# A decoder layer on one core: four weight sums move to VectorE, one projection moves up in TensorE's order

## The chip, the cores and the metric

The kernel runs on one NeuronCore of a Trainium2 chip. The metric is the device time of one execution in microseconds. The engines are TensorE (PE), ScalarE (ACT), VectorE (DVE), GpSimd (POOL) and SyncE (SP), which issues every DMA of this kernel.

## What is computed

One decoder layer for 8 batches of 512 tokens and 256 channels:

```python
x = x + attn(layernorm(x))            # one head of 128; 512 keys
x = x + xattn(layernorm(x), ctx)      # relu(x W + b), relu(ctx W + b), masked softmax, times ctx
x = x + ffn(layernorm(x))             # 256 -> 1024 -> 256, quantised activations and weights

def weight_quant(w):                  # w_gate, w_up, w_down
    scale = 1.0 / clip(mean(abs(w)), 1e-5)
    return clip(round(w * scale), -1, 1) / scale
```

The change concerns `mean(abs(w))` of the three FFN weights, and the first three batches of `attn`.

## The kernel before

Each batch goes through three streams, in steps that have a letter and a batch number. `A` is self-attention: Q, K, V, VT (V transposed), S0 to S3 (scores of four groups of 128 queries), P0 to P3 (their exponentials transposed), H (P times V) and Y0, Y1 (H times the output weight, added to x). `E` projects the context: YP0 and YP1. `B` is cross-attention and `C` the FFN. `W` and `F` prepare weights: `F.sum0` to `F.sum5` sum |w| of the two halves of gate, up and down, `F.total` is the matmul with ones that adds them over the partitions (it needs all six), `F.sc` the small VectorE operations behind it, `F.round` and `F.sign` make the ternary weights on GpSimd and ScalarE.

The order of the work on every engine is written out by hand: `PE_ORDER`, `ACT_ORDER`, `DVE_ORDER`, `POOL_ORDER` and `SP_ORDER` are strings of steps, `run()` walks through them, and semaphores join the engines. An engine executes its list in order, so a step that waits holds up all that stands behind it in the list.

Exact products are made of two f32r halves. A step such as `A.Q/2` is six f32r matmuls on TensorE (L1070 to L1072); ScalarE then rounds the high half out of the PSUM bank (L835) and VectorE takes the low half (L1460); only then may the bank be filled again. Which bank an A or E step fills comes from `a_tables()`: a list of banks for the first steps, one for `A_NEXT` (the rest of the second batch), and then `a0` and `a1` in turn, while E steps from the third batch on use bank `e`:

```python
def a_step(step, n):
    dst = a_bank(step, n)
    if A_BEFORE[step, n]:
        a_read(*A_BEFORE[step, n])     # wait until the bank's last step has been read
```

Batch 0 differs: its x, context and W are used as they are loaded, without halves (`A.Q/0` is 4 matmuls in f32, `E.YP0/0` waits for the loads of W and of the context, L1158 on). Its key scale `r_bc` comes from a matmul `W.r` of a diagonal and ScalarE's copy (L848, `r0_set`), which the first score step and `A.V/0` on VectorE wait for. Every relu of YP (L888, L889) takes the bias, which comes with `W.o`, one load of 129.5 KB that also holds w_o and the head mask (`small_loaded`). VectorE's `W.wo0` (L1624) waits for the same load. For batch n > 0 `r_bc` goes by DRAM: SP stores a_rstd (`S.rw`) and loads it back to all partitions (`S.rb`).

The sum of one half of a weight is one ScalarE activation with an accumulator:

```python
def prep_sum(j):
    act.wait_ge(ffn_loaded[j // 2], 16)
    if j > 0:
        act.wait_ge(w_sums, j)
    act.activation(gateT..., ffn_raw[j // 2][:, ...], ACT.Abs,
                   accum_out=w_sum[:, j % 2, j // 2:j // 2 + 1]).then_inc(w_sums, 1)
```

Of the kernel before, what the change touches and what calls it, by code (L numbers as in the profile page):

```python
# [79 lines left out]
DVE_DN = [(n, t) for n in range(8) for t in range(4) if (n, t) not in POOL_DN]  # L80
SILU = [(6, j) for j in range(4, 8)] + [(7, j) for j in range(8)]
# [7 lines left out]
    A.P0/2 A.S2/2 B.P3/0 B.O2/0 A.P1/2 A.S3/2 B.O3/0 B.XT0/1 A.P2/2 A.P3/2 E.YP0/3 B.XT1/1 A.H/2 B.XP0/1 B.XP1/1
    E.YP1/3 A.Y0/2 A.Y1/2 C.g0/0 C.u0/0 A.Q/3 B.S0/1 B.S1/1 C.g1/0 C.u1/0 B.P0/1 B.S2/1 C.u2/0 C.g2/0 A.K/3  # L90
    A.V/3 B.P1/1 C.u3/0 C.g3/0 B.O0/1 B.S3/1 B.P2/1 C.g4/0 C.u4/0 E.YP0/4 C.g5/0 B.O1/1 C.u5/0 B.P3/1 B.O2/1
    A.VT/3 A.S0/3 B.O3/1 C.g6/0 C.u6/0 E.YP1/4 B.XT0/2 B.XT1/2 C.g7/0 C.DN0/0 C.u7/0 A.S1/3 A.P0/3 B.XP0/2
    B.XP1/2 A.S2/3 C.DN1/0 C.u0/1 C.g0/1 A.P1/3 A.S3/3 B.S0/2 B.S1/2 C.g1/1 C.u1/1 B.P0/2 B.S2/2 C.DN2/0 C.g2/1
    C.u2/1 C.DN3/0 B.P1/2 B.O0/2 A.P2/3 A.P3/3 C.g3/1 C.u3/1 B.S3/2 B.P2/2 C.g4/1 A.H/3 B.O1/2 B.P3/2 C.u4/1
    A.Y0/3 A.Y1/3 C.g5/1 C.u5/1 A.Q/4 A.K/4 C.u6/1 B.O2/2 B.O3/2 C.DN0/1 C.g6/1 B.XT0/3 B.XT1/3 A.V/4 E.YP0/5
    A.VT/4 A.S0/4 C.g7/1 C.u7/1 B.XP0/3 B.XP1/3 A.S1/4 A.P0/4 C.DN1/1 C.g0/2 A.S2/4 C.u0/2 C.DN2/1 A.P1/4 A.S3/4
    C.g1/2 C.u1/2 B.S0/3 B.S1/3 C.g2/2 C.u2/2 E.YP1/5 A.P2/4 A.P3/4 C.g3/2 C.u3/2 C.DN3/1 B.P0/3 B.S2/3 C.g4/2
    A.H/4 C.u4/2 B.P1/3 C.g5/2 B.O0/3 B.S3/3 A.Y0/4 A.Y1/4 B.P2/3 C.g6/2 C.u5/2 B.O1/3 B.P3/3 A.Q/5 A.K/5 C.u6/2
    B.O2/3 B.O3/3 A.V/5 B.XT0/4 B.XT1/4 C.g7/2 C.DN0/2 A.VT/5 A.S0/5 C.u7/2 B.XP0/4 C.DN1/2 A.S1/5 B.XP1/4
    A.P0/5 A.S2/5 C.u0/3 C.g0/3 C.DN2/2 C.u1/3 B.S0/4 C.g1/3 B.S1/4 A.P1/5 A.S3/5 B.P0/4 B.S2/4 C.g2/3 C.DN3/2  # L100
    C.u2/3 B.P1/4 B.O0/4 C.g3/3 B.S3/4 A.P2/5 A.P3/5 C.u3/3 B.P2/4 B.O1/4 C.u4/3 A.H/5 C.g4/3 E.YP0/6 A.Y0/5
    A.Y1/5 B.P3/4 C.u5/3 C.g5/3 B.O2/4 A.Q/6 A.K/6 B.O3/4 C.g6/3 C.u6/3 A.V/6 B.XT0/5 B.XT1/5 E.YP1/6 C.u7/3
    C.g7/3 A.VT/6 A.S0/6 B.XP0/5 C.u0/4 C.g0/4 B.XP1/5 C.DN0/3 C.g1/4 C.u1/4 C.DN1/3 A.S1/6 A.P0/6 B.S0/5 B.S1/5
    C.g2/4 A.S2/6 A.P1/6 B.P0/5 C.DN2/3 C.u2/4 A.S3/6 B.S2/5 C.u3/4 C.DN3/3 C.g3/4 B.P1/5 B.O0/5 A.P2/6 A.P3/6
    C.u4/4 C.g4/4 B.S3/5 B.P2/5 A.H/6 B.O1/5 C.g5/4 C.u5/4 A.Y0/6 A.Y1/6 B.P3/5 B.O2/5 C.g6/4 A.Q/7 A.K/7 C.u6/4
    B.O3/5 A.V/7 C.DN0/4 C.u7/4 A.VT/7 A.S0/7 B.XT0/6 B.XT1/6 E.YP0/7 C.g7/4 A.S1/7 A.P0/7 B.XP0/6 B.XP1/6
    A.S2/7 A.P1/7 C.g0/5 C.u0/5 C.DN1/4 A.S3/7 C.g1/5 B.S0/6 B.S1/6 A.P2/7 C.u1/5 A.P3/7 B.P0/6 B.S2/6 A.H/7
    C.g2/5 B.P1/6 B.O0/6 C.u2/5 A.Y0/7 A.Y1/7 C.u3/5 C.g3/5 B.S3/6 B.P2/6 E.YP1/7 C.g4/5 B.O1/6 C.u4/5 B.P3/6
# [7 lines left out]
    A.Q/0 W.qkv/0 W.hi/0 A.xT0/1 E.ctxT/1 A.xT1/1 W.r/0 E.YP0/0 A.VT/0 W.wo/0 F.sum0/0 A.exp0/0 A.exp1/0
    A.exp2/0 E.YP1/0 A.exp3/0 A.P0/0 A.Q/1 A.P2/0 A.K/1 F.sum1/0 F.sum2/0 E.YP0/1 A.xT0/2 A.xT1/2 F.sum3/0 A.H/0
    A.VT/1 F.sum4/0 F.sum5/0 A.exp0/1 E.YP1/1 A.P0/1 E.ctxT/2 A.exp1/1 A.exp2/1 A.exp3/1 A.P1/1 A.P2/1 A.P3/1
    B.mask/0 E.YP0/2 B.norm0/0 B.norm1/0 A.H/1 B.XT0/0 B.XT1/0 B.ctx/0 F.sign0/0 F.sign1/0 B.XP0/0 B.XP1/0
    E.YP1/2 A.Q/2 A.K/2 B.exp0/0 B.exp1/0 B.P0/0 E.ctxT/3 A.VT/2 B.P1/0 A.xT0/3 A.xT1/3 B.exp2/0 A.exp0/2 B.P2/0  # L120
    B.exp3/0 A.exp1/2 B.mask/1 A.P0/2 B.P3/0 B.norm0/1 B.norm1/1 A.P1/2 A.exp2/2 A.exp3/2 A.P2/2 A.P3/2
    C.norm0/0 B.XT0/1 B.XT1/1 F.sign2/0 F.sign3/0 E.YP0/3 F.sign4/0 A.H/2 F.sign5/0 B.XP0/1 B.XP1/1 C.t0/0
    C.u0/0 B.ctx/1 E.YP1/3 C.norm1/0 B.exp0/1 A.Q/3 C.t1/0 C.u1/0 B.P0/1 C.u2/0 C.t2/0 B.exp1/1 E.ctxT/4
    B.exp2/1 B.P1/1 B.norm0/2 A.K/3 C.t3/0 C.u3/0 A.xT0/4 B.P2/1 C.t4/0 B.exp3/1 B.mask/2 C.u4/0 C.hb0/0
    B.norm1/2 C.u5/0 B.P3/1 A.xT1/4 C.t5/0 E.YP0/4 C.norm0/1 A.VT/3 C.u6/0 C.t6/0 C.hb1/0 B.XT0/2 B.XT1/2
    A.exp0/3 C.t7/0 C.u7/0 A.P0/3 B.ctx/2 B.XP0/2 B.XP1/2 A.exp1/3 A.exp2/3 C.u0/1 C.t0/1 C.hb2/0 C.hb3/0
    B.exp0/2 C.t1/1 B.P0/2 C.u1/1 B.exp1/2 C.norm1/1 A.exp3/3 A.P1/3 B.exp2/2 B.P1/2 C.t2/1 C.u2/1 A.P2/3 A.P3/3
    C.t3/1 C.u3/1 E.ctxT/5 B.P2/2 C.t4/1 E.YP1/4 B.exp3/2 A.H/3 C.hb0/1 C.u4/1 C.u5/1 B.P3/2 C.norm0/2 A.Q/4
    A.K/4 C.t5/1 B.norm0/3 B.norm1/3 B.mask/3 B.XT0/3 B.XT1/3 C.t6/1 C.u6/1 C.hb1/1 C.hb2/1 A.VT/4 B.ctx/3
    C.t7/1 C.u7/1 A.exp0/4 B.XP0/3 B.XP1/3 A.P0/4 A.exp1/4 C.norm1/2 C.t0/2 C.u0/2 A.P1/4 E.YP0/5 C.t1/2 C.hb3/1  # L130
    C.u1/2 A.exp2/4 A.exp3/4 C.t2/2 C.u2/2 B.exp0/3 B.exp1/3 A.P2/4 A.P3/4 C.t3/2 C.u3/2 B.P0/3 C.t4/2 A.xT0/5
    A.xT1/5 A.H/4 C.u4/2 B.P1/3 C.t5/2 B.exp2/3 E.ctxT/6 C.hb0/2 B.P2/3 B.exp3/3 E.YP1/5 B.P3/3 C.u5/2 A.Q/5
    A.K/5 B.norm0/4 C.u6/2 B.mask/4 C.t6/2 B.norm1/4 C.hb1/2 B.XT0/4 B.XT1/4 C.norm0/3 C.t7/2 C.hb2/2 A.VT/5
    B.ctx/4 C.u7/2 A.exp0/5 B.XP0/4 B.XP1/4 A.P0/5 C.u0/3 C.t0/3 C.norm1/3 A.exp1/5 C.u1/3 C.hb3/2 B.exp0/4
    C.t1/3 A.xT0/6 A.xT1/6 B.P0/4 B.exp1/4 C.t2/3 A.P1/5 A.exp2/5 B.P1/4 A.exp3/5 B.exp2/4 C.t3/3 C.u2/3 A.P2/5
    A.P3/5 C.u3/3 B.P2/4 C.u4/3 B.exp3/4 A.H/5 B.mask/5 C.t4/3 C.norm0/4 C.hb0/3 C.hb1/3 C.t5/3 B.P3/4 E.YP0/6
    C.u5/3 A.Q/6 B.norm0/5 B.norm1/5 A.K/6 B.ctx/5 C.t6/3 C.u6/3 B.XT0/5 B.XT1/5 A.xT0/7 A.xT1/7 C.t7/3 A.VT/6
    C.u7/3 C.norm1/4 C.u0/4 C.t0/4 B.XP0/5 B.XP1/5 A.exp0/6 C.u1/4 C.t1/4 A.P0/6 C.hb2/3 C.hb3/3 A.exp1/6
    B.exp0/5 B.exp1/5 B.P0/5 C.t2/4 A.P1/6 C.u2/4 C.u3/4 A.exp2/6 A.exp3/6 C.t3/4 B.P1/5 A.P2/6 A.P3/6 B.exp2/5
    C.t4/4 C.hb0/4 C.u4/4 E.YP1/6 B.P2/5 A.H/6 E.ctxT/7 C.t5/4 B.exp3/5 B.P3/5 C.u5/4 B.mask/6 C.t6/4 A.Q/7  # L140
# [1583 lines left out]
```

## Time and profile before

| | |
|---|---|
| time, median of 3 runs | 372.63 us (371.84 to 372.91) |
| the profiled execution: its time, its span | 372.06 us, 370.1 us |
| busy: PE, ACT, DVE, POOL | 98%, 86%, 85%, 79% of the span |
| TensorE clock granted | full (1.0) |
| DMA | 36.92 MB, mean 100 GB/s |
| chain that ended last | PE 76%, POOL 6%, ACT 5%, DMA 4%, DVE 3% |

The span runs from the first to the last instruction of the profiled execution; the time of that execution is 1.96 us longer. Timeline rows give the start and the duration of an instruction (or of some merged ones, x their number) and in brackets how long the engine sat idle before it and what released it. Busy time of a pipelined matmul includes overlap with the next one: successive 128x512 f32r matmuls start 0.23 us apart though each is shown as 0.39 us long.

### The profile page before, as it was taken

The page shows a single profiled execution, that of the slowest core. Times are in us where ns is not written, and L with a number is a line of the kernel's source. Part 1 is how long each engine was busy: PE and PEld are TensorE (multiplying, and loading weights), DVE is VectorE, ACT ScalarE, POOL GpSimd, SP SyncE. Part 2 cuts the span into 40 slices and gives each one's busy share as a digit, 9 for nine tenths or more (in the row PEclk, how much of TensorE's full clock was granted, in tenths as well). Part 3 has the DMA queues.
Part 4 walks back from the last instruction along what each step waited for, and adds up shares of the span by engine and source line. Part 5 has one row for each costly group of instructions (what it writes and reads, how often), then busy time and mean ns, then how long its engine had stood idle before and what let it go on. Part 6 is the DMA issues. An engine that isn't in the chain of part 4 may idle for free.

```text
span 370.1 us, 7362 instructions
## 1 busy us (share of the span) xinstructions
PE 361.5 (98%) x2116; PEld 280.2 (76%) x2116; DVE 313.8 (85%) x918; ACT 318.6 (86%) x590; POOL 294.0 (79%) x421
## 2 busy tenths in 40 slices
...
DMA packets 47735, 36.92 MB, mean 100 GB/s; under 512 B 39248, under 2 KB 40912, under 8 KB 47312
## 3 DMA queue, kind: packets, MB, share of 16 engines
...
q14 instruction: 22, 0.18, 0.2%
...
## 4 chain that ended last, share of the span: by engine, by line
PE 76%; POOL 6%; ACT 5%; DMA 4%; DVE 3%; issue 3%; SPq 1%; POOLq 0%; ACTq 0%; DVEq 0%
PE b_bank L1070 8%; PE b_bank L1071 8%; PE b_bank L1072 8%; PE a_bank L1070 6%; PE a_bank L1072 6%; PE a_bank L1071 6%; PE g_bank L1284 5%; PE d_bank L1304 5%; PE u_bank L1284 5%; PE b_bank L1212 3%; DMA x_all<-in_x 2%; PE a_bank L1132 2%; PE b_bank L1183 2%; POOL c_work L703 1%; POOL xp_lo L656 1%
## 5 line engine op out<-in xcount | busy, mean ns | idle before, releaser
L703 POOL TENSOR_TENSOR c_work<-c_work 128x512 f32<-128x512 f32 x48 | 61.8, 1297 | 3.4 <-DVE c_work L1540 2.4
L960 ACT ACTIVATE c_work<-g_bank,c_tanh_scale 128x512 f32<-128x512 f32 x52 | 35.9, 690 | 5.8 <-PE g_bank L1284 3.3
L1070 PE MATMUL b_bank<-ctx_hi,b_pT_hi 128*128 128x256 f32 x128 | 39.2, 307 | 0.0
L1540 DVE SCALAR_TENSOR_TENSOR c_work<-c_work,g_bank 128x512 f32<-128x512 f32 x50 | 33.9, 678 | 6.1 <-ACT c_work L960 5.7
L1071 PE MATMUL b_bank<-ctx_lo,b_pT_hi 128*128 128x256 f32 x128 | 36.1, 282 | 0.0
L1072 PE MATMUL b_bank<-ctx_hi,b_pT_lo 128*128 128x256 f32 x128 | 36.0, 282 | 0.0
L963 ACT ACTIVATE c_work<-u_bank 128x512 f32<-128x512 f32 x48 | 28.9, 601 | 8.2 <-PE u_bank L1284 8.2
L1284 PE MATMUL g_bank<-gateT,xqT 128*128 128x512 bf16 x112 | 33.6, 382 | 0.9 <-ACT xqT L935 0.5
L750 POOL TENSOR_SCALAR c_work<-c_work,h_q 128x1024 f32<-128x1024 f32 x28 | 31.7, 1132 | 3.2 <-DVE h_q L1574 3.2
L1284 PE MATMUL u_bank<-upT,xqT 128*128 128x512 bf16 x112 | 33.5, 381 | 0.6 <-DVE c_work L1535 0.6
L1567 DVE TENSOR_REDUCE h_max<-c_work 128x1 f32<-128x1024 f32 x26 | 31.4, 1206 | 1.1 <-POOL c_work L703 1.1
L1304 PE MATMUL d_bank<-downT,c_half 128*128 128x256 bf16 x240 | 31.2, 273 | 0.2 <-DMA c_half<-c_half 0.2
L1304 PEld LDWEIGHTS d_bank<-downT,c_half 128*128 128x128 bf16 x240 | 22.7, 98 | 8.5 <-issue 2.7
L651 POOL TENSOR_TENSOR yp_lo<-e_relu,yp_hi 128x512 fp32r<-128x512 f32 x16 | 20.7, 1295 | 10.2 <-ACT yp_hi L889 10.2
L970 ACT ACTIVATE c_half<-c_work 128x1024 bf16<-128x1024 f32 x26 | 27.3, 1056 | 0.5 <-POOL c_work L750 0.5
L1070 PE MATMUL b_bank<-yp_hi,xp_hi 128*128 128x512 f32 x64 | 27.4, 429 | 0.1
L1070 PEld LDWEIGHTS b_bank<-ctx_hi,b_pT_hi 128*128 128x128 f32 x128 | 24.3, 190 | 1.8 <-issue 0.2
L643 POOL TENSOR_TENSOR a_xT_lo<-a_xT_raw,a_xT_hi 128x512 fp32r<-128x512 f32 x14 | 18.4, 1316 | 8.6 <-ACT a_xT_hi L844 8.6
L1072 PE MATMUL b_bank<-yp_hi,xp_lo 128*128 128x512 f32 x64 | 25.2, 394 | 0.0
L898 ACT ACTIVATE b_p<-b_p,b_nmax 128x512 f32<-128x512 f32 x32 | 23.1, 723 | 2.5 <-DVE b_nmax L1516 2.4
L1071 PE MATMUL b_bank<-yp_lo,xp_hi 128*128 128x512 f32 x64 | 25.1, 391 | 0.0
L1516 DVE CUSTOM_DVE_ANT_0 b_p<-b_bank,mask_add 128x512 f32<-128x512 f32 x32 | 21.8, 683 | 3.7 <-PE b_bank L1072 3.6
...
## 6 DMA issues: line engine op xcount, KB each, us to landing
ctx_raw<-in_ctx SPq DMA_DIRECT2D x8, 512.0 KB, 4.5
a_xT_raw<-in_x_t SPq DMA_DIRECT2D x7, 512.0 KB, 4.4
ctxT_raw<-in_ctx_t SPq DMA_DIRECT2D x7, 512.0 KB, 5.4
x_all<-in_x SPq DMA_DIRECT2D x7, 512.0 KB, 3.8
out<-x_all SPq DMA_DIRECT2D x7, 512.0 KB, 2.9
...
c_work<-in_w_gate SPq DMA_DIRECT2D x1, 1024.0 KB, 10.9
c_work<-in_w_up SPq DMA_DIRECT2D x1, 1024.0 KB, 12.6
```

The costliest lines, as they stand in the source:

```text
L703: pool.tensor_tensor(h[:, t % 2, half * HALF:(half + 1) * HALF], th[:, j % 2, :], up[:, j % 2, :], ALU.mult).then_inc(hs, 1)
L750: pool.tensor_scalar(h_tile(t, n), h_tile(t, n), h_q[:, t:t + 1], ROUND if n < LAST else ROUND_F16, ALU.mult, ALU.add).then_inc(h_rounds, 1)
L960: act.activation(gate_tile(j, n), gu_bank("g", j, n), ACT.Silu if (n, j) in SILU else ACT.Tanh, scale=c_tanh_scale[:, j // 2:j // 2 + 1]). ...
L963: act.activation(up[:, j % 2, :], gu_bank("u", j, n), ACT.Copy).then_inc(ups, 1)
L970: act.activation(h_q8[:, t % 2, :], h_tile(t, n), ACT.Copy, bias=-ROUND).then_inc(hqs, 1)
L1070: pe.matmul(dst, l_hi, r_hi, start=first, stop=False)
L1071: pe.matmul(dst, l_hi, r_lo, start=False, stop=False)
L1072: return pe.matmul(dst, l_lo, r_hi, start=False, stop=last)
L1284: mm = pe.matmul(dst, xqT[:, t * DC + c, :], w[:, c, cols], start=c == 0, stop=c == DC - 1)
L1304: mm = pe.matmul(dn_bank(t, n)[:, 0:D], h_T[:, t % 2, f, :], downT[:, f, :], start=f == 0, stop=f == FC - 1)
L1540: dve.scalar_tensor_tensor(gate_tile(j, n), gate_tile(j, n), 1.0, gu_bank("g", j, n), ALU.add, ALU.mult).then_inc(gates, 1)
L1567: dve.tensor_reduce(h_max[:, one], h_tile(t, n), AX.X, ALU.max, apply_absolute_value=True).then_inc(h_maxes, 1)
```

## The change

Four of the six sums (up and down) become VectorE reductions with their own semaphore; `F.total` waits for both. `A.Q/2` enters `A_NEXT` between `P1/1` and `P2/1` and fills bank `e`, and with it the turn of `a0` and `a1` is shifted by one for all later A steps. The five order strings are written anew over roughly the first third of the work; from there to the end they are as before.

```diff
-A_NEXT = "S3/1 P1/1 P2/1 P3/1 H/1 Y0/1 Y1/1"
+A_NEXT = "S3/1 P1/1 Q/2 P2/1 P3/1 H/1 Y0/1 Y1/1"
-SECOND_BANKS = ["u", "d", "a0", "a1", "g", "u", "d"]
+SECOND_BANKS = ["u", "d", "e", "a0", "a1", "g", "u", "d"]
     later = [f"{step}/{n}" for n in range(2, 8) for step in A_STEPS.split()]
+    later = [entry for entry in later if entry not in A_NEXT.split()]
+DVE_SUMS = [2, 3, 4, 5]
+ACT_SUMS = [m for m in range(6) if m not in DVE_SUMS]
...
             def prep_sum(j):
                 act.wait_ge(ffn_loaded[j // 2], 16)
-                if j > 0:
-                    act.wait_ge(w_sums, j)
+                if ACT_SUMS.index(j) > 0:
+                    act.wait_ge(w_sums, ACT_SUMS.index(j))
...
                 elif name == "total":
-                    pe.wait_ge(w_sums, 6)
+                    pe.wait_ge(w_sums, len(ACT_SUMS))
+                    pe.wait_ge(dve_w_sums, len(DVE_SUMS))
...
+            def prep_sum(j):
+                dve.wait_ge(ffn_loaded[j // 2], 16)
+                dve.tensor_reduce(w_sum[:, j % 2, j // 2:j // 2 + 1], ffn_raw[j // 2][:, (j % 2) * F:(j % 2 + 1) * F], AX.X, ALU.add,
+                                  apply_absolute_value=True).then_inc(dve_w_sums, 1)
```

In step names: on ScalarE `A.exp1/1` now follows `A.exp0/1` directly (two sums, `E.YP1/1`, `A.P0/1` and `E.ctxT/2` stood before it), `B.mask/0` and `B.ctx/0` come ahead of `A.exp0/1`, and the first `E.YP0/0` stands before `A.exp0/0`. On GpSimd the a_rstd steps of batch 1 come ahead of `E.ctxT/1`. On SP `S.ctx/0`, `S.ctxT/2` and `S.xT/2` stand between `S.rw/1` and `S.rb/1`.

The start of SyncE's list, the loads in the order in which they are issued (`wo_and_small` is the load with the bias, `b_xn` here holds the transposed context of batch 0, `a_xT_raw`, `ctxT_raw` and the second `x_all` belong to batch 1). Before:

```order
L580 DMA x_all<-in_x 128x512 x2
L591 DMA wo_and_small<-in_w_o_b_mask 128x259
L587 DMA xqT<-in_W 128x512
L585 DMA b_xn<-in_ctx_t 128x1024
L524 DMA a_xT_raw<-in_x_t 128x1024
L543 DMA ctxT_raw<-in_ctx_t 128x1024
L550 DMA mask_u8<-in_mask 128x512
L512 DMA x_all<-in_x 128x1024
L594 DMA c_work<-in_w_gate 128x2048
L594 DMA c_work<-in_w_up 128x2048
```

Now:

```order
L582 DMA x_all<-in_x 128x512
L552 DMA mask_u8<-in_mask 128x512
L582 DMA x_all<-in_x 128x512
L589 DMA xqT<-in_W 128x512
L526 DMA a_xT_raw<-in_x_t 128x1024
L514 DMA x_all<-in_x 128x1024
L545 DMA ctxT_raw<-in_ctx_t 128x1024
L587 DMA b_xn<-in_ctx_t 128x1024
L596 DMA c_work<-in_w_gate 128x2048
L593 DMA wo_and_small<-in_w_o_b_mask 128x259
L596 DMA c_work<-in_w_up 128x2048
```

The mask went between the halves of batch 0's x, batch 1's x went up by two large loads, the context of batch 0 went down by two, and the bias load went behind gate.

VectorE around `A.V/0` (`vT<-g_bank`) and the first scores (the ISA rows), with `W.wo0` (`hm_f`). Before:

```order
L1631 TENSOR_TENSOR wt_lo<-xqT,wt_hi 128x512
L1624 CAST hm_f<-wo_and_small 128x1
L1355 BN_STATS a_bn<-x_all 128x6 x4
L1491 TENSOR_TENSOR vT<-g_bank,r_bc 128x512
L1362 BN_AGGR a_mv<-a_bn 128x2 x2
L1479 ISA a_p,a_max<-e_bank,r_bc,a_rstd 128x512
L1479 ISA a_max 128x1
L1479 ISA a_p,a_max<-b0_bank,r_bc,a_rstd 128x512
```

Now:

```order
L1358 BN_STATS a_bn<-x_all 128x6 x4
L1365 BN_AGGR a_mv<-a_bn 128x2 x4
L1482 ISA a_p,a_max<-e_bank,r_bc,a_rstd 128x512
L1482 ISA a_max 128x1
L1494 TENSOR_TENSOR vT<-g_bank,r_bc 128x512
L1639 TENSOR_TENSOR wt_lo<-xqT,wt_hi 128x512
L1632 CAST hm_f<-wo_and_small 128x1
L1482 ISA a_p,a_max<-b0_bank,r_bc,a_rstd 128x512
```

The first score of batch 0 stands ahead of `A.V/0`, and `hm_f`, which needs the bias load, between the first and the second score. The sums of `up` follow after the fourth score, those of `down` after `A.P3/0`.

TensorE around `A.P1/1`, the first transpose row in each. Before:

```order
L1132 MATMUL d_bank<-ident,a_p 128x128 x4
L1327 MATMUL b1_bank<-w_sum,ones 128x3 x2
L1132 MATMUL a0_bank<-ident,a_p 128x128 x4
L1132 MATMUL a1_bank<-ident,a_p 128x128 x4
L1070 MATMUL e_bank<-ctxT_hi,wt_hi 128x512
L1071 MATMUL e_bank<-ctxT_lo,wt_hi 128x512
```

Now:

```order
L1134 MATMUL d_bank<-ident,a_p 128x128 x4
L1072 MATMUL e_bank<-a_xT_hi,wqkv_hi 128x512
L1073 MATMUL e_bank<-a_xT_lo,wqkv_hi 128x512
L1074 MATMUL e_bank<-a_xT_hi,wqkv_lo 128x512
L1072 MATMUL e_bank<-a_xT_hi,wqkv_hi 128x512
L1073 MATMUL e_bank<-a_xT_lo,wqkv_hi 128x512
L1074 MATMUL e_bank<-a_xT_hi,wqkv_lo 128x512
L1134 MATMUL a0_bank<-ident,a_p 128x128 x4
L1330 MATMUL b1_bank<-w_sum,ones 128x3 x2
L1134 MATMUL a1_bank<-ident,a_p 128x128 x4
L1072 MATMUL e_bank<-ctxT_hi,wt_hi 128x512
```

The six matmuls of `A.Q/2` stand behind `A.P1/1`, and `E.YP0/2` (the last row) fills the same bank `e` behind them.

## Rows read from the trace of the kernel before

**Rows 1.** The page: span, and busy time of each engine
```profile
span 370.1 us, 7362 instructions
PE 361.5 (98%) x2116; PEld 280.2 (76%) x2116; DVE 313.8 (85%) x918; ACT 318.6 (86%) x590; POOL 294.0 (79%) x421
```

**Rows 2.** TensorE's timeline: start, duration, operation, idle before and releaser
```profile
17.37 0.66 PE L1116 MATMUL u_bank<-ident,vT 128*128 128x128 f32 x4 [1.01 <-DVE vT L1491]
...
21.30 0.60 PE L1132 MATMUL e_bank<-ident,a_p 128*128 128x128 f32 x4
...
39.74 0.63 PE L1132 MATMUL d_bank<-ident,a_p 128*128 128x128 f32 x4 [1.05 <-ACT a_p L867]
...
41.53 0.48 PE L1070 MATMUL e_bank<-ctxT_hi,wt_hi 128*128 128x512 f32 x1
...
42.55 0.40 PE L1071 MATMUL e_bank<-ctxT_lo,wt_hi 128*128 128x512 f32 x1
42.78 0.39 PE L1072 MATMUL e_bank<-ctxT_hi,wt_lo 128*128 128x512 f32 x1
43.55 0.47 PE L1070 MATMUL g_bank<-a_pT_hi,b_pT_hi 128*128 128x512 f32 x1 [0.38 <-DVE a_pT_lo L1464]
...
137.17 0.60 PE L1284 MATMUL g_bank<-gateT,xqT 128*128 128x512 bf16 x2 [0.21 <-DMA xqT<-xq]
```

**Rows 3.** ScalarE's timeline
```profile
13.01 1.06 ACT L919 ACTIVATE ctxT_hi<-ctxT_raw 128x1024 fp32r<-128x1024 f32 x1 [0.59 <-DMA ctxT_raw<-in_ctx_t]
...
14.49 0.58 ACT L848 ACTIVATE r_bc<-b_bank 128x512 f32<-128x512 f32 x1
...
18.96 1.04 ACT L859 ACTIVATE gateT<-c_work 128x1024 f32<-128x1024 f32 x1
...
20.00 0.71 ACT L867 ACTIVATE a_p<-a_p,a_nmax 128x512 f32<-128x512 f32 x1
...
35.52 0.71 ACT L867 ACTIVATE a_p<-a_p,a_nmax 128x512 f32<-128x512 f32 x1
...
38.79 0.72 ACT L867 ACTIVATE a_p<-a_p,a_nmax 128x512 f32<-128x512 f32 x1
```

**Rows 4.** VectorE's timeline
```profile
16.64 0.67 DVE L1491 TENSOR_TENSOR vT<-g_bank,r_bc 128x512 f32<-128x512 f32 x1
...
24.09 0.18 DVE L1656 RECIPROCAL a_inv<-a_sum 128x4 f32<-128x4 f32 x1 [2.99 <-ACT a_p L867]
...
32.88 0.69 DVE L1468 TENSOR_TENSOR hT_lo<-d_bank,hT_hi 128x512 fp32r<-128x512 f32 x1 [4.57 <-ACT hT_hi L838]
...
42.13 1.28 DVE L1464 TENSOR_TENSOR a_pT_lo<-a_bank,a_pT_hi 128x512 fp32r<-128x512 f32 x2
...
55.32 0.69 DVE L1460 SCALAR_TENSOR_TENSOR q_lo<-a_bank,q_hi 128x512 fp32r<-128x512 f32 x1 [1.37 <-ACT q_hi L835]
```

**Rows 5.** SyncE's timeline: when loads were issued
```profile
5.70 0.44 SPq L550 DMA_DIRECT2D mask_u<-in_mask  x1
6.19 0.65 SPq L512 DMA_DIRECT2D x_all<-in_x  x1
6.88 0.71 SPq L594 DMA_DIRECT2D c_work<-in_w_gate  x1
7.63 0.44 SPq L594 DMA_DIRECT2D c_work<-in_w_up  x1
```

**Rows 6.** DMA issues of 0 to 30 us: KB each, median us to landing
```profile
c_work<-in_w_gate SPq DMA_DIRECT2D x1, 1024.0 KB, 10.9
c_work<-in_w_up SPq DMA_DIRECT2D x1, 1024.0 KB, 12.6
...
x_all<-in_x SPq DMA_DIRECT2D x1, 512.0 KB, 9.1
...
mask_u<-in_mask SPq DMA_DIRECT2D x1, 64.0 KB, 7.9
```

**Rows 7.** The page's groups: busy, mean ns, idle before
```profile
L1567 DVE TENSOR_REDUCE h_max<-c_work 128x1 f32<-128x1024 f32 x26 | 31.4, 1206 | 1.1 <-POOL c_work L703 1.1
```

More of the change, by code:

```diff
@@ L89 @@
[L89 to L108, printed above, removed]
```

232 lines of the change are left out of this document (126 added, 106 removed).

## The prediction

> **What bounds the kernel now.** I read the page first. TensorE is busy 361.5 of 370.1 us, and no other engine passes 86% [rows 1]. A busy share alone doesn't prove a bound, so the second view is TensorE's timeline, row by row. Inside a step the f32r matmuls start 0.23 us apart (42.55, 42.78) though each is drawn 0.39 us long [rows 2]: the drawn length includes 0.16 us of overlap, and the next matmul is always there to start. The third view is the list of TensorE's waits. Between 16 us and 137 us it has three entries: 1.01 us before 17.37 (the transpose of V of batch 0, released by VectorE), 1.05 us before 39.74 (`A.P1/1`, released by ScalarE's exponential) and 0.38 us before 43.55 (`A.H/1`, released by VectorE); the next is 0.21 us at 137.17 [rows 2]. The chain of waits agrees: 76% of it is TensorE.
>
> So the change, which takes no work from TensorE, can win only what TensorE waits, or lose by new waits. The ceiling: 1.01 + 1.05 + 0.38 = 2.44 us, and at each wait the 0.16 us of overlap is lost too, 0.48 us: **2.9 us**. All of it lies ahead of 44 us.
>
> The Trainium skill, Perfetto Trace Analysis, Identifying the Most-Contended Engine, says that matmul busy time is a bad measure of TensorE's headroom and that the busy share of weight loads should be used instead; by it there would be room here. The weight loads are at 76% [rows 1]. I hold with the spacing of the starts; what the other reading would give is a rival below.
>
> **Part 1: the loads and the start of batch 0.** The first wait of TensorE is for `A.V/0` on VectorE, which ran at 16.64 for 0.67 us [rows 4], behind the statistics of batch 1's x. That x landed at 6.19 + 9.1 = 15.3 us [rows 5, 6], though the scale `r_bc` that V needs was ready at 14.49 + 0.58 = 15.07 [rows 3]. Now batch 1's x is issued two large loads earlier. Loads land nearly in the order of issue: gate at 6.88 + 10.9 = 17.8, up at 7.63 + 12.6 = 20.2, so 1024 KB take 2.4 us and 512 KB 1.2 us [rows 5, 6]; x should land near 12 and its statistics be done by 14. Then `r_bc` decides. Ahead of its copy ScalarE has the same kinds of work as before (the transposed context of batch 1, which waited for its load until 13.01, and one 128x512 copy), so 15.07 stands if that load does. VectorE then takes the first score (0.68, about the 0.67 of V's row) and V, both at 0.6 to 0.7 us: done at about 16.4 instead of 17.3, a gain of 0.9 us.
>
> Against it stands the mask, now ahead of all large loads. It landed at 5.70 + 7.9 = 13.6, which is 0.6 us behind the context load of 13.01, and the x behind it needed 1.7 us more instead of 1.2 [rows 3, 5, 6]. So mask and x can bring 0 to 1.0 us of delay to whatever stands behind them, the context of batch 1 among them. I take 0.3: **gain 0.6 us**, bounds -0.1 and 0.9.
>
> The bias load moves behind gate. The bytes up to its end are those up to gate's end before, so it should land at about 17.8 to 18.0. ScalarE's two relus of `E.YP0/0` (two 128x512 passes, 1.2 us together) then end at 19.2 and the first exponential starts there, against 20.00 before, when `F.sum0` (18.96 to 20.00, 1.04 us) stood in that place [rows 3]. TensorE's `A.P0/0` stood at 21.30 [rows 2], would now stand at 20.7 and needs the exponential, done at 19.9: 0.8 us of cover. VectorE's `hm_f` waits for the same load, and the second score, at about 18.0 in both orders, behind it.
>
> **Part 2: the sums.** A reduction of 128x1024 on VectorE costs 1.21 us [rows 7], four cost 4.8 us; ScalarE gives up four of 1.04 us [rows 3]. The sums of up stand where VectorE was idle 2.99 us before 24.09, those of down where it was idle 4.57 us before 32.88 [rows 4]. The first pair can start when up has landed (20.2) and the fourth score is done (about 20.5) and pushes the copy of `A.P1/0` to some 23.4 to 24.1, where it was; the second ends near 29.5. TensorE needs nothing of VectorE in between but `A.V/1`, for the transpose behind `A.H/0`, at about 31. Cost: **0**. If that cover is gone (V/1 also waits for the reload of `r_bc`, which now has three loads of 512 KB ahead of it, 3.6 us behind the weights' end at about 22.6, so some 26.3 and the broadcast itself), each us beyond 30.3 costs one. On ScalarE 4.2 us go, but it is not the bound: **0** by itself.
>
> **Part 3: batch 1 and the moved Q.** `A.exp1/1` came at 38.79, 3.27 us behind `A.exp0/1` at 35.52 [rows 3], because four steps stood between. Now it follows at once, so the 1.05 us wait of `A.P1/1` goes. What is late next is VectorE. From 32.88 (`hT_lo`) to 42.13 + 1.28 = 43.41 (the low halves of P2 and P3) it works almost without a pause, 10.5 us, and all of it hangs on `A.H/0` [rows 4]. Its list keeps all this work and gets the low half of Q/2, 0.69 us in its row [rows 4], 0.6 between starts. With the gain g of part 1 it ends at 44.0 - g; the half of Q/2, which stands ahead of those of P2 and P3 (1.2 us), at 42.8 - g. On TensorE Q/2 takes 6 x 0.23 = 1.4 us. It fills the time of the old wait, but `E.YP0/2` fills the same bank `e` behind it and has to wait for VectorE: from 42.8 - g to 44.2 - g. Then `A.H/1` starts; P3's half is there. Before, H/1 started at 43.55 and Q/2 was still to come. Gain: 43.55 + 1.4 - (44.2 - g) = **0.75 + g**. So of the 1.4 us that the moved Q could hide about half is given back as a new wait of 0.5 to 1.2 us on bank `e`. Q/2's place behind `A.Y1/1` is taken by V/2, which needs nothing new.
>
> **Part 4: the rest to the end.** The reordered stretch reaches to about 115 us, and behind it the lists are as before. TensorE had no wait from 44 to 137 us, and the steps that feed it have 1.4 us less to come in. ScalarE is better placed there (sums gone; context, mask and sign steps earlier), VectorE as before. I count 0, with bounds of -0.5 and +0.3 (the waits at 137 and in the tail).
>
> **Sum:** 0.75 + 0.6 = 1.35 us. The profiled execution took 372.06 us (span 370.1 and 1.96 around it) and would take 370.7. The median of the runs is 0.57 us above the profiled one, so the forecast for the median is 372.63 - 1.35 = **371.3 us**, with a range of its own from 370.6 (g at its upper bound, tail +0.3) to 372.0 (g near 0).
>
> **Rivals.**
> 1. *Both waits vanish and none comes.* For it: ScalarE's exponentials are much earlier. Against it: VectorE's 10.5 us run. It gives the ceiling, 372.63 - 2.9 = 369.7 us. Chance 0.15.
> 2. *The waits only move.* The mask costs the whole 1.0 us (g = -0.1), and the new waits on P2/1, P3/1 and bank `e` take most of the rest. 372.63 - 0.4 = 372.2 us. For it: the mask's row. Chance 0.17.
> 3. *TensorE was not the bound, ScalarE was.* Then the four sums come off the time: 4 x 1.04 = 4.2, giving 368.4 us. Against it: TensorE's starts are 0.23 us apart without a gap. This is what the page cited above would suggest. Chance 0.03.
> 4. *Slower: the bias load comes late.* It stands behind the 1024 KB of gate in a full queue. If it lands at t, the exponential is done at t + 1.9 and `A.P0/0` starts then, so g = 21.3 - (t + 1.9) = 19.4 - t as soon as t passes 18.8, and the gain is 20.15 - t. It decides from t = 20.15, which is up's landing; landing with down (about 22.6) it costs 2.45 us: 375.1 us. For it: `hm_f` and the relus both block lists. Against it: other loads landed in order. Chance 0.10.
>
> **How the numbers follow.** The forecast has 0.55. A measurement of this kernel can tell about 0.3%, 1.1 us, from no change, so faster means below 371.5. The forecast's own range lies on that side for 0.6 of its weight: 0.33, and rivals 1 and 3 add 0.18: faster 0.51. Slower by over 0.3% (above 373.7) is rival 4 past t = 21.3, and some room for a wait that I don't see: 0.09. The same: 0.40. The range runs from 369.7 (rival 1) to 373.0, which takes in rival 2 and the mild end of rival 4; about 0.15 is left out.
>
> **What would show it.** In the changed profile: TensorE's transposes of V/0 start 0.5 to 1.0 us earlier with a wait that is short or gone; `A.P0/0` near 20.7; the wait for ScalarE's exponential before `A.P1/1` is gone; a new wait of 0.5 to 1.2 us before `E.YP0/2`, released by VectorE's low half of Q; `A.H/1` near 43.6 with Q/2 done; four reductions of 1.2 us on VectorE without anyone waiting; landing of the bias by 18.8. Wrong would be: a wait of VectorE or ScalarE for the bias beyond that, a wait of TensorE on `A.V/1`'s transpose (the reload), or new waits of TensorE between 50 and 130 us.

## The result and the profile after

The changed kernel takes **373.69 us** (median of 20 runs, 372.05 to 374.75), the kernel before 372.13 us beside it (20 runs, 371.09 to 375.31). The ratio is 1.0033, with a 95% interval from 1.0017 to 1.005: slower by 1.2 us, by the medians by 1.56 us, where I had forecast a gain of 1.35 us. The profiled execution has a span of 371.7 us against 370.1.

The page of the changed kernel, the lines that answer to [rows 1]:

```profile
span 371.7 us, 7326 instructions
PE 360.4 (97%) x2088; PEld 280.6 (75%) x2116; DVE 319.1 (86%) x922; ACT 314.5 (85%) x582; POOL 294.0 (79%) x421
```

TensorE's timeline of the changed kernel (it answers to [rows 2]; L1082 is `A.V/0`, L1324 `W.r`, the first L1134 row `A.P0/0`, the second `A.P1/1`, L1072 into bank `e` `E.YP0/2`, L1072 into `g` `A.H/1`):

```profile
11.72 1.98 PE L1082 MATMUL g_bank<-c_xn,b_p 128*128 128x512 f32 x4 [1.73 <-DVE b_p L1622]
15.26 1.13 PE L1324 MATMUL b_bank<-vT,ones 128*128 128x512 f32 x2 [1.56 <-DVE vT L1370]
...
23.53 0.60 PE L1134 MATMUL e_bank<-ident,a_p 128*128 128x128 f32 x4
...
40.78 0.60 PE L1134 MATMUL d_bank<-ident,a_p 128*128 128x128 f32 x4
...
44.79 0.49 PE L1072 MATMUL e_bank<-ctxT_hi,wt_hi 128*128 128x512 f32 x1 [0.42 <-DVE q_lo L1463]
...
46.29 0.39 PE L1072 MATMUL g_bank<-a_pT_hi,b_pT_hi 128*128 128x512 f32 x1
```

The second half of this is what was forecast: the wait before `A.P1/1` is gone, a short one on bank `e` has come. The first half is not. `A.V/0` and `W.r`, which no term of my sum touches, are late. The same two steps before:

```profile
9.33 1.98 PE L1080 MATMUL g_bank<-c_xn,b_p 128*128 128x512 f32 x4
11.80 1.13 PE L1322 MATMUL b_bank<-vT,ones 128*128 128x512 f32 x2 [0.48 <-DVE vT L1367]
```

So `A.V/0` starts 2.39 us late and `W.r` 3.46 us. VectorE's timeline of the changed kernel says why in its first row: the statistics of the second half of batch 0's x wait 2.18 us for its load. The centring of V's weights (`b_p`, L1622) stands behind them in VectorE's list, and `A.V/0` waits for that. (Before this wait the matmuls of Q and K start 0.49 us late, at 6.39 instead of 5.90. That is scatter: of two kernels below that differ in nothing up to there, one starts them at 5.63 and one at 6.64.)

```profile
10.26 0.75 DVE L1358 BATCH_NORM_STATS2 a_bn<-x_all 128x6 f32<-128x256 f32 x2 [2.18 <-DMA x_all<-in_x]
10.93 0.37 DVE L1365 BATCH_NORM_AGGREGATE a_mv<-a_bn 128x2 f32<-128x6 f32 x4
11.21 0.46 DVE L1622 SCALAR_TENSOR_TENSOR b_p<-u_bank,b_p 128x128 f32<-128x128 f32 x2
...
13.45 1.75 DVE L1370 TENSOR_TENSOR vT<-ident,a_rstd 128x512 f32<-128x512 f32 x1
```

The last row is a second surprise: the spread of the scales, which feeds `W.r`, takes 1.75 us. Before, it took 0.69, and all four statistics were one row at 7.22:

```profile
7.22 1.41 DVE L1355 BATCH_NORM_STATS2 a_bn<-x_all 128x6 f32<-128x256 f32 x4 [1.08 <-DMA x_all<-in_x]
...
11.06 0.69 DVE L1367 TENSOR_TENSOR vT<-ident,a_rstd 128x512 f32<-128x512 f32 x1
```

SyncE's timeline of the changed kernel: the mask is issued at 2.58, and the issue at 4.47 takes 2.19 us, its neighbours 0.43.

```profile
2.58 0.43 SPq L552 DMA_DIRECT2D mask_u<-in_mask  x1
3.05 0.43 SPq L582 DMA_DIRECT2D x_all<-in_x  x1
...
4.47 2.19 SPq L514 DMA_DIRECT2D x_all<-in_x  x1
```

Its stretches of 1 us (busy time of PE, PEld, DVE, ACT, POOL with instructions, granted clock, DMA share, GB/s): three slices at 216, 172 and 286 GB/s.

```profile
5.00:6.00 1.00, 1.00 (x7) 1.00 (x6) 0.57 (x3) 0.00 (x0) 0.00 (x0) 1.00 0.69 216
6.00:7.00 1.00, 1.00 (x6) 0.76 (x6) 0.40 (x2) 0.00 (x0) 0.00 (x0) 1.00 0.65 172
7.00:8.00 1.00, 1.00 (x3) 0.40 (x3) 0.68 (x2) 0.00 (x0) 0.00 (x0) 1.00 0.83 286
```

The kernel before has 358, 235 and 331 GB/s there.

From this came **theory M**: the mask's load, 512 bytes that go to all 128 partitions, holds up what is behind it by some 2 us. **Theory P**: the long spread comes from GpSimd, which takes the low halves of xT/1 (batch 1's transposed x) meanwhile. The rival to both: the sums, the moved Q or VectorE's long run cost the time, and the late start is only a shift.

### The profile page after: what moved, and what is told of

It reads as the page before. It is cut to its first block, busy times and chain, and to the rows that moved or that the text cites. A ratio compares the mean times of both kernels' runs of the same rounds, so it can differ in the third digit from the quotient of the medians.

```text
span 371.7 us, 7326 instructions
## 1 busy us (share of the span) xinstructions
PE 360.4 (97%) x2088; PEld 280.6 (75%) x2116; DVE 319.1 (86%) x922; ACT 314.5 (85%) x582; POOL 294.0 (79%) x421
## 4 chain that ended last, share of the span: by engine, by line
PE 81%; POOL 4%; ACT 4%; DMA 4%; DVE 3%; issue 3%; SPq 1%; ACTq 0%; POOLq 0%; DVEq 0%
PE b_bank L1072 9%; PE b_bank L1074 9%; PE b_bank L1073 9%; PE a_bank L1074 6%; PE a_bank L1072 6%; PE a_bank L1073 6%; PE g_bank L1286 5%; PE u_bank L1286 5%; PE d_bank L1306 5%; PE b_bank L1214 3%; PE a_bank L1134 2%; DMA x_all<-in_x 2%; PE b_bank L1185 2%; PE e_bank L1072 2%; PE e_bank L1073 2%
## 5 line engine op out<-in xcount | busy, mean ns | idle before, releaser
L1072 PE MATMUL b_bank<-ctx_hi,b_pT_hi 128*128 128x256 f32 x128 | 39.3, 307 | 0.0
L1286 PE MATMUL u_bank<-upT,xqT 128*128 128x512 bf16 x103 | 31.6, 381 | 1.1 <-DVE c_work L1538 0.6
L1286 PE MATMUL g_bank<-gateT,xqT 128*128 128x512 bf16 x93 | 29.4, 381 | 2.1 <-ACT xqT L937 0.5
L1072 PE MATMUL b_bank<-yp_hi,xp_hi 128*128 128x512 f32 x64 | 28.0, 437 | 0.1
L1072 PEld LDWEIGHTS b_bank<-ctx_hi,b_pT_hi 128*128 128x128 f32 x128 | 24.3, 190 | 2.3 <-issue 0.6
L1073 PEld LDWEIGHTS b_bank<-ctx_lo,b_pT_hi 128*128 128x128 f32 x128 | 24.4, 190 | 0.5
L869 ACT ACTIVATE a_p<-a_p,a_nmax 128x512 f32<-128x512 f32 x32 | 23.1, 728 | 1.5 <-DVE a_nmax L1487 1.4
```

Of the source, the lines that this page charges most:

```text
L1072: pe.matmul(dst, l_hi, r_hi, start=first, stop=False)
L1073: pe.matmul(dst, l_hi, r_lo, start=False, stop=False)
L1286: mm = pe.matmul(dst, xqT[:, t * DC + c, :], w[:, c, cols], start=c == 0, stop=c == DC - 1)
```

## The experiments

Each kernel ran 12 times (the one called "the same row" 6 times) and was timed against the kernel before on its own chip; ratios are those. The medians of the kernel before were 371.95 us beside mask late, mask alone, no overlap and bias in the slot; 371.83 beside distinct rows, Q back, sums back and both repairs; 372.11 beside the same row, the mask on ScalarE's queue, sums alone and Q's low half first. The profile is of one execution, and its time can lie 1.3 us off the median; where it does, the text says so.

### Undoing one part at the start

**Mask late.** The changed kernel with

```diff
-    W.x0/0 S.mask/0 W.x1/0 W.W/0 S.xT/1 S.x/1 S.ctxT/1 W.c/0 F.gate/0
+    W.x0/0 W.x1/0 W.W/0 S.xT/1 S.x/1 S.ctxT/1 W.c/0 S.mask/0 F.gate/0
```

> The changed kernel with only the mask's load moved: from between the two halves of x0 to behind the bias c, ahead of gate. Theory M (the mask's load, which writes one 512-byte row to each of 128 partitions, holds up whatever stands behind it by some 2 us, and with x0's second half the centring of V, the transposes of A.V/0, the scale row W.r and A.P0/0): x0's second half lands by 8.3 us instead of 10.26, A.V/0 starts on TensorE by 9.6 instead of 11.7, W.r near 12.5 instead of 15.3, A.P0/0 near 21 instead of 23.5, and the time falls by 2.2 to 2.9 us below the changed kernel, to 370.8 to 371.5, below the kernel before. Rival (the sums, the moved Q or VectorE's long run are the cost and the start is only shifted): within 0.5 us of the changed kernel, 373.2 to 373.9.

Measured: 370.92 us, ratio 0.9967 (0.9948 to 0.9986). TensorE's timeline:

```profile
9.88 1.88 PE L1082 MATMUL g_bank<-c_xn,b_p 128*128 128x512 f32 x4
...
21.41 0.63 PE L1134 MATMUL e_bank<-ident,a_p 128*128 128x128 f32 x4
```

`A.V/0` starts 1.84 us earlier than in the changed kernel, without a wait, and `A.P0/0` 2.12 us. Both are 0.3 to 0.4 us behind what I expected; the spread still takes 1.75 us. Moving one load of 64 KB gives back 2.5 us by the ratios, and what is left of the change beats the kernel before. The rival that the start is only a shift falls.

**The mask alone**, in the kernel before:

```diff
-    W.x0/0 W.x1/0 W.o/0 W.W/0 W.c/0 S.xT/1 S.ctxT/1 S.mask/0 S.x/1
+    W.x0/0 S.mask/0 W.x1/0 W.o/0 W.W/0 W.c/0 S.xT/1 S.ctxT/1 S.x/1
```

> The kernel before with one edit: the mask's load moved ahead of x0's second half, as in the changed kernel. Theory M: x0's second half lands near 10.2 us instead of 7.7, the first transposes of V start near 11.7 instead of 9.3, and the time rises by 2.0 to 2.8 us, to 374.2 to 375.0. Rival (the mask's place costs only in company with the rest of the new load order): within 0.5 us of the kernel before, 371.7 to 372.6.

Measured: 372.31 us, ratio 1.0002 (0.9981 to 1.0023). That is the rival's range, and theory M's 2.0 to 2.8 us are not there. The start is late all the same. TensorE's timeline (of the slowest of the 12 executions, 373.57 us):

```profile
11.21 1.98 PE L1080 MATMUL g_bank<-c_xn,b_p 128*128 128x512 f32 x4 [1.14 <-DVE b_p L1614]
13.68 1.12 PE L1322 MATMUL b_bank<-vT,ones 128*128 128x512 f32 x2 [0.49 <-DVE vT L1367]
...
18.07 0.60 PE L1116 MATMUL u_bank<-ident,vT 128*128 128x128 f32 x4
```

`A.V/0` and `W.r` are 1.88 us late, but the wait of 1.01 us before the transpose of V [rows 2] is gone: batch 1's x lands late there anyway, and the late start runs into that slack. `A.P0/0` stands at 21.95, 0.65 us behind. So the mask holds up the loads in both kernels, and what that costs depends on the rest of the order of loads, as the rival said. The change brought batch 1's x earlier and put the mask in front with the same edit, so it had no such slack left to cover the mask.

**No overlap.** The changed kernel with a wait ahead of GpSimd's first low half of xT/1:

```diff
                 pool.wait_ge(xT_his, DC * (n - 1) + c + 1)
+                if n == 1 and c == 0:
+                    pool.wait_ge(r0_spread, 1)
```

> The changed kernel with one wait added: GpSimd's low halves of xT/1 (128x512 each, 1.6 us) start only when VectorE has spread the scales (the operation at 13.45 us that took 1.75 us where it took 0.69 before). Theory P (the two engines' overlap made it long): it takes 0.7 us, W.r starts near 14.2 instead of 15.26, the time falls by about 1.0 us against the changed kernel, to 372.7. Rival (it is long for a reason of its own, or something behind it takes the gain): it still takes over 1.5 us and the time stays within 0.3 us of the changed kernel. The halves of xT/1 end later by about 1 us, at 17.5, ahead of their first user on TensorE by more than that, so no loss is expected from them.

Measured: 371.78 us, ratio 0.9985 (0.9964 to 1.0005), 1.8 us below the changed kernel by the ratios, where I expected 1.0. In the profiled executions the spans are 1.4 us apart (370.3 and 371.7) and `A.P0/0` is 1.32 us earlier, 0.25 of which is the load, 10.01 instead of 10.26. VectorE's and GpSimd's timelines:

```profile
13.20 0.68 DVE L1372 TENSOR_TENSOR vT<-ident,a_rstd 128x512 f32<-128x512 f32 x1
```
```profile
14.03 2.51 POOL L647 TENSOR_TENSOR a_xT_lo<-a_xT_raw,a_xT_hi 128x512 fp32r<-128x512 f32 x2 [1.43 <-DVE vT L1372]
```

In the changed kernel GpSimd's pair had begun 0.31 us ahead of the spread, and both were slow together, 3.20 instead of 2.51 and 1.75 instead of 0.68:

```profile
13.14 3.20 POOL L645 TENSOR_TENSOR a_xT_lo<-a_xT_raw,a_xT_hi 128x512 fp32r<-128x512 f32 x2 [0.29 <-ACT a_xT_hi L846]
```

### What about the mask holds the queue

**Bias in the slot.** Mask late, and the bias load (129.5 KB, 128 rows too) in the mask's place:

```diff
-    W.x0/0 S.mask/0 W.x1/0 W.W/0 S.xT/1 S.x/1 S.ctxT/1 W.c/0 F.gate/0 W.o/0 F.up/0
+    W.x0/0 W.o/0 W.x1/0 W.W/0 S.xT/1 S.x/1 S.ctxT/1 W.c/0 S.mask/0 F.gate/0 F.up/0
```

> As the kernel with the mask late (mask behind c), but the bias load of W.o, whose rows are longer, stands in the slot between x0's halves that the mask had. If the count and the small size of the mask's descriptors are what holds the queue: x0's second half lands by 8.5 us and the time is within 0.3 us of the mask-late kernel. If any load in that slot costs as much: x0's second half lands beyond 9.3 us and the time is within 0.6 us of the changed kernel.

Measured: 371.04 us, ratio 0.9967 (0.9946 to 0.9988); x0's second half is used at 8.28, as expected. Neither the slot nor the bytes are the cost.

**Distinct rows.** Mask late plus one more load in the slot, into a tile that nothing reads:

```diff
+                elif name == "d":
+                    sp.dma_start(spare[:, :], w_gate[:, 0, 0:P]).then_inc(spare_loaded, 16)
```

> The mask-late kernel (370.92 us) with one load added in the slot between x0's halves: 64 KB in 128 rows of 512 bytes, as the mask's, but read from 128 different places of w_gate; it writes a tile that nothing reads. If what holds the queue is that the mask's 128 rows are all read from the same 512 bytes: x0's second half lands by 8.4 us and the time is 370.7 to 371.4. If rows of 512 bytes in themselves do: it lands beyond 9.3 us and the time is 372.4 to 373.9.

Measured: 371.02 us, ratio 0.9976 (0.9958 to 0.9995). The statistics start at 6.68 and run through without a wait for the second half. By the ratios this is 0.3 us above mask late, less than the intervals can tell: 128 rows of 512 bytes have no price here that shows.

**The same row.** The same kernel, except for the source:

```diff
-                    sp.dma_start(spare[:, :], w_gate[:, 0, 0:P])...
+                    sp.dma_start(spare[:, :], w_gate[0, 0, 0:P].partition_broadcast(P))...
```

> The mask-late kernel (370.92 us) with a 64 KB load in the slot between x0's halves, as in the distinct-rows kernel (371.02 us), except that all 128 rows are read from the same 512 bytes of w_gate. Theory S (128 reads of one place of the memory hold the queue): x0's second half lands at 9.3 us or later, A.V/0 starts beyond 11 us, and the time is 372.3 to 373.9. Rival (something of the mask itself, its type or its tensor): x0's second half by 8.4 us, 370.7 to 371.4.

Measured: 374.22 us, ratio 1.006 (1.0039 to 1.0081), by the medians 3.2 us above the distinct rows. VectorE's timeline has the wait again:

```profile
9.62 0.75 DVE L1362 BATCH_NORM_STATS2 a_bn<-x_all 128x6 f32<-128x256 f32 x2 [1.85 <-DMA x_all<-in_x]
```

The DMA issues of 0 to 30 us, KB and us to landing, of the distinct rows and then of the same row:

```profile
spare<-in_w_gate SPq DMA_DIRECT2D x1, 64.0 KB, 4.3
```
```profile
spare<-in_w_gate SPq DMA_DIRECT2D x1, 64.0 KB, 6.4
```

The two kernels differ in nothing but whether 128 reads of 512 bytes go to 128 places or to one. That decides: 2.1 us later to land, and 3.2 us in time. It is not a matter of more pieces, both profiles count 3025 packets from 0 to 30 us; where in the memory or the DMA engines the repeated reads are held is not shown. The Trainium skill, DMA: Bandwidth & Descriptors, Rules for kernel authors, advises to join many small transfers into a large one, since under 64 KB one pays mostly overhead. That goes by size, and the two loads have the same size, 64 KB: it can't tell 4.3 us from 6.4, so it is not what made the mask dear.

**The mask on ScalarE's queue**, issued at that engine's start:

```diff
+            act.dma_start(mask_u8[:, 0, :], mask[0, :].partition_broadcast(P)).then_inc(mask_loaded, 16)
```

> The changed kernel with the mask's load issued from ScalarE's queue at its start instead of SP's. If the mask blocks only what stands behind it in the same queue: x0's second half lands by 8.3 us and the time is 370.6 to 371.5, as with the mask late. If it takes the memory or the DMA engines for as long as it runs: some load of the start is late by 1 us or more again, A.V/0 starts beyond 10.8 us, and the time is over 372.

Measured: 373.51 us, ratio 1.0034 (1.0016 to 1.0053). x0 is in time for everything, but now the first load of all is late; TensorE's timeline (of the fastest of the 12 executions, 372.16 us, so it can't account for the whole of the median):

```profile
5.98 1.19 PE L1320 MATMUL b_bank<-b_p,ones 128*128 128x128 f32 x4 [2.08 <-DMA b_p<-in_w_qkv]
```

`w_qkv` lands at 0.72 + 5.1 = 5.8 us instead of 3.7, and the two loads of `c_xn` behind it take 5.4 us instead of 3.9. So the load doesn't only block what stands behind it in its own queue: loads that move at the same time on SyncE's queue are late by 1.5 to 2.1 us.

### The other two parts

**Q back.** The bias-slot kernel with `A.Q/2` at its old place and `A_NEXT` and `SECOND_BANKS` as before:

```diff
-    A.P1/1 A.Q/2 A.P2/1 F.total/0 ... A.Y1/1 A.K/2
+    A.P1/1 A.P2/1 F.total/0 ... A.Y1/1 A.Q/2 A.K/2
```

> The bias-slot kernel (371.04 us) with Q/2 back at its old place behind Y1/1, in its old bank. Theory Q (the prediction's part 3: the moved Q fills TensorE's time between A.P1/1 and A.H/1, in which VectorE's low halves are late): a wait of 0.5 to 1.4 us comes back on TensorE ahead of A.P2/1, A.P3/1 or A.H/1, and the time rises by 0.4 to 1.2 us, to 371.4 to 372.2. Rival (the exponential's new place alone made the gain, the moved Q only shifts work): within 0.3 us of 371.04.

Measured: 373.32 us, ratio 1.0028 (1.001 to 1.0047), 2.3 us above the bias-slot kernel by the ratios. TensorE has its wait again, now one step on, before `A.P2/1`:

```profile
39.85 0.63 PE L1132 MATMUL a_bank<-ident,a_p 128*128 128x128 f32 x4 [1.52 <-ACT a_p L867]
```

From `A.P1/1` (1.07 us earlier than in the bias-slot kernel, 37.74 against 38.81) to `A.H/1` with Q/2 counted in (42.82 + 1.4 = 44.2 against 44.31) this costs 1.0 us. Up to there the earlier start pays for it. Another 1.1 us are lost behind, a little in a wait of 0.20 us at 55.54, so that the spans are 1.0 us apart (370.8 against 369.8). The medians are 2.3 us apart, about twice the most I expected, and I have no row for all of it.

The start of this profiled execution shows theory P without an edit of GpSimd's work. VectorE's spread came first, by 0.12 us:

```profile
10.62 0.68 DVE L1368 TENSOR_TENSOR vT<-ident,a_rstd 128x512 f32<-128x512 f32 x1
```
```profile
10.74 2.94 POOL L643 TENSOR_TENSOR a_xT_lo<-a_xT_raw,a_xT_hi 128x512 fp32r<-128x512 f32 x2 [0.72 <-ACT a_xT_hi L844]
```

Now VectorE is at its 0.68 and GpSimd pays, 2.94 us instead of 2.51. The Trainium skill, SBUF — State Buffer, Who interferes with whom, has this as a rule: a VectorE instruction with two inputs in SBUF contends with a GpSimd instruction that reads SBUF, the port pair that they share is an exclusive lock, and the order of issue decides who is blocked. The traces agree: in the changed kernel VectorE's excess, 1.07 us, is about what GpSimd's running instruction had left (half of the undisturbed 2.51 is 1.26 us, 0.31 were gone, which leaves 0.95), and GpSimd's excess, 0.69 us, is the length of VectorE's instruction.

**Sums back.** The bias-slot kernel with all six sums on ScalarE, at their old places:

```diff
-DVE_SUMS = [2, 3, 4, 5]
+DVE_SUMS = []
-    F.sum1/0 E.YP0/1 A.xT0/2 A.xT1/2 B.mask/0 A.H/0 A.VT/1 B.ctx/0 A.exp0/1
+    F.sum1/0 F.sum2/0 E.YP0/1 A.xT0/2 A.xT1/2 F.sum3/0 B.mask/0 A.H/0 A.VT/1 F.sum4/0 F.sum5/0 B.ctx/0 A.exp0/1
```

> The bias-slot kernel (371.04 us) with all six sums of |w| on ScalarE again, the four at the places they had in the kernel before. Theory (part 2 of the prediction: the sums cost nothing on either engine by themselves): within 0.3 us of 371.04. Rival A (the four sums on ScalarE, 4.2 us, push its exponentials of batch 1 behind TensorE's need): a wait of TensorE on ScalarE of 0.5 us or more between 24 and 41 us and a time over 371.5. Rival B (the sums on VectorE cost time in the changed kernel): below 370.6.

Measured: 373.15 us, ratio 1.0031 (1.001 to 1.0051), 2.4 us above the bias-slot kernel by the ratios: rival A. TensorE's timeline has three stalls, two of them for ScalarE's exponential:

```profile
34.30 0.35 PE L1070 MATMUL u_bank<-wo_hi,hT_hi 128*128 128x256 f32 x1 [0.74 <-issue]
...
38.03 0.63 PE L1132 MATMUL a_bank<-ident,a_p 128*128 128x128 f32 x4 [0.70 <-ACT a_p L867]
...
42.50 0.63 PE L1132 MATMUL a_bank<-ident,a_p 128*128 128x128 f32 x4 [0.60 <-ACT a_p L867]
```

**Sums alone.** The kernel before with the four sums on VectorE and nothing else moved:

```diff
-    A.N3/0 A.inv/0 A.P1/0 A.Q/1 A.K/1 A.P3/0 A.V/1
+    A.N3/0 F.sum2/0 F.sum3/0 A.inv/0 A.P1/0 A.Q/1 A.K/1 A.P3/0 F.sum4/0 F.sum5/0 A.V/1
```

> The kernel before with one part of the change: four of the sums on VectorE, at the places where it was idle, nothing else moved. Theory A (from the run with the sums back: ScalarE's sums are what made its exponential of batch 1 late): TensorE's wait of 1.05 us before A.P1/1 goes or halves, and the time falls by 0.3 to 1.2 us, to 370.6 to 371.5. Rival (part 2 of the prediction: the sums are worth nothing by themselves, the order of the exponentials is): the wait stays at about 1 us and the time within 0.3 us of the kernel before.

Measured: 372.82 us, ratio 1.002 (0.9997 to 1.0044). No gain: by the ratio 0.7 us above the kernel before, outside the rival's 0.3, but the interval reaches down to no change. The rival's mechanism holds, TensorE's wait has not moved:

```profile
40.41 0.63 PE L1131 MATMUL d_bank<-ident,a_p 128*128 128x128 f32 x4 [1.04 <-ACT a_p L866]
```

Together: moving the sums is worth nothing where `A.exp1/1` stands behind three other steps (the prediction miscounted them as four), and 2.4 us where it follows at once and the mask and context steps are ahead of it. The move of the sums and the new order of ScalarE are one measure; neither is priced alone.

### Towards a better version

**Both repairs**: bias in the slot, mask late, and the no-overlap wait.

> The bias-slot kernel (mask behind c, bias load in its old slot, 371.04 us) with the wait of the no-overlap kernel added: GpSimd's low halves of xT/1 start when VectorE has spread the scales. Theory P (the overlap with GpSimd costs the chain 1.07 us): the spread takes 0.7 us instead of 1.75, W.r starts near 12.2 instead of 13.28, A.P0/0 near 20.5 instead of 21.55, the time is 0.8 to 1.1 us lower, 369.9 to 370.2. Rival (something else, as the context of batch 1 on ScalarE, holds the scale row's copy then): A.P0/0 gains less than 0.4 us and the time stays above 370.6.

Measured: **370.38 us**, ratio 0.9952 (0.9929 to 0.9974), the lowest of all, below the kernel before by 1.8 us by the ratio and by 1.45 by the medians. Against bias in the slot it is 0.6 us by the ratios, less than the 0.8 to 1.1 expected, and the two intervals overlap, so the second repair shows in the times only on top of the changed kernel. In the profile it shows here too: the spread takes 0.68 us and `A.P0/0` stands at 20.20 instead of 21.55:

```profile
12.04 1.02 PE L1326 MATMUL b_bank<-vT,ones 128*128 128x512 f32 x2
...
20.20 0.60 PE L1136 MATMUL e_bank<-ident,a_p 128*128 128x128 f32 x4
```

The first matmuls of Q and K, in bias in the slot and then in both repairs, which have the same work up to there, show how much a single start can scatter:

```profile
5.63 3.76 PE L1082 MATMUL a_bank<-c_xn,b_p 128*128 128x512 f32 x8
```
```profile
6.64 3.84 PE L1084 MATMUL a_bank<-c_xn,b_p 128*128 128x512 f32 x8
```

**Q's low half first**, in that kernel:

```diff
-    A.P1/1 B.ag1/0 A.Q/2 A.P2/1
+    A.Q/2 A.P1/1 B.ag1/0 A.P2/1
```

> The kernel with the bias slot and without the overlap (370.38 us, the best so far) with VectorE's low half of Q/2 moved ahead of those of P1/1. TensorE's wait of 0.42 us on bank e before E.YP0/2 should shrink or go; at most 0.42 + 0.16 = 0.6 us lower, 369.8 to 370.2, if nothing takes its place. Rival: the low half of Q/2 now waits for TensorE's Q/2 and holds P1/1's, P2/1's and P3/1's behind it, A.H/1 waits instead, and the time stays at 370.2 to 370.8.

Measured: 370.87 us, ratio 0.9973 (0.9957 to 0.9989), no gain. The wait grew from 0.42 to 1.01 us, and VectorE now idles 0.76 us for ScalarE's high half of Q:

```profile
41.37 0.50 PE L1073 MATMUL e_bank<-ctxT_hi,wt_hi 128*128 128x512 f32 x1 [1.01 <-DVE a_pT_lo L1468]
```

It is released by the low half of P1/1, not of Q: the kernel has TensorE wait for a count of low halves, Q/2's place in TensorE's order, so the place in VectorE's list doesn't bring the release forward. The edit didn't test what I meant it to.

## Why the prediction was wrong

**What bounds the kernel: right.** TensorE does. ScalarE gave up 4.1 us and the time rose, so rival 3 is out.

**Part 1: this step failed.** "So mask and x can bring 0 to 1.0 us of delay to whatever stands behind them, the context of batch 1 among them", of which I took 0.3. The delay is 2.39 us, read at `A.V/0`; moving the mask away took 1.84 of it, and the other 0.55 is of the size of the scatter of the first matmuls. I bounded it by the landings of the mask where it stood before, which say how long it took, not what it held up; around 13.6 us the kernel before loses no throughput (419 GB/s from 13 to 14 us). And I took the context of batch 1 as what stands behind it, though the rows of the order show the second half of x0 directly there. ScalarE's copy `r_bc` was done at 17.03 (16.43 + 0.60), not at 15.1 to 15.4 [rows 3]. The path that I did watch was late by far more than 0.3 us too. ScalarE's timeline:

```profile
14.66 1.06 ACT L921 ACTIVATE ctxT_hi<-ctxT_raw 128x1024 fp32r<-128x1024 f32 x1 [0.60 <-DMA ctxT_raw<-in_ctx_t]
...
16.43 0.60 ACT L850 ACTIVATE r_bc<-b_bank 128x512 f32<-128x512 f32 x1 [0.19 <-PE b_bank L1324]
```

The context of batch 1 is used 1.65 us later than before (14.66 against 13.01), and by that alone ScalarE would have come to `r_bc` only at 16.24. The second part of the miss has no term at all: 1.07 us in the spread, from GpSimd's low halves that the new order of loads brought forward into it. Together 3.46 us at `W.r`; TensorE's wait for V (1.01 + 0.16) is gone as forecast, and `A.P0/0` stands at 23.53 instead of 21.30: g is -2.2, outside the bounds of -0.1 and 0.9.

**The bias: nearly right.** It landed at 8.53 + 10.2 = 18.7 us, where I had 17.8 to 18.0 from [rows 5, 6], and with the late start nobody waited for it, so rival 4, my only slow case, did not occur. With the mask late it does bite a little: ScalarE's relu waits 0.54 us for it until 19.30.

**Part 2: right in size, wrong in reach.** The reductions took 1.21 us each, as in [rows 7], nobody waited for them, and `A.V/1` at 32.05 was in time. But "On ScalarE 4.2 us go, but it is not the bound: **0** by itself" holds only in the old order, as the two runs with the sums show.

**Part 3: right.** The formula put `A.H/1` at 44.2 - g; with the measured g of -2.23 that is 46.4, and it stood at 46.29. Against g the gain is 43.55 + 1.4 - 46.29 + 2.23 = 0.89 us, forecast 0.75. The wait on bank `e` is 0.42 us, a little under the 0.5 to 1.2, released by `q_lo` as said. **Part 4**: from +1.34 us at `A.H/1` to +1.6 in the span, so another 0.26 us are lost where I counted 0, inside the bounds.

Put the measured g into the sum and it gives 0.75 - 2.23, so 1.5 us slower; the medians say 1.56 and the ratio 1.2. With both faults of the start removed, and with the bias load in another place than in the change, the kernel is 1.45 to 1.8 us faster, where the forecast was 1.35.
